# A two-layer graph network on one core: layer 0's sums taken node by node over pairs of tiles, and the first chunk of stage three normalised ahead of the barrier

## The chip, the core and the metric

The kernel runs on one core of a Trainium2 chip. Time is device microseconds (us) of one execution. Of the core's engines TensorE (PE, with its weight loads as PEld) multiplies matrices into PSUM, VectorE (DVE), ScalarE (ACT) and GpSimd (POOL) do the rest, and SyncE (SP) issues most of the DMAs.

## The reference

3125 nodes with 128 features, 103125 edges sorted by destination, everything in float32. Two layers follow each other:

```python
h = relu(layernorm(x))
# layer 0
neighbour = h[dst] @ W_N.T + b_N
agg = segment_sum(neighbour * exp(-edge_weight)[:, None], src)
x = x + relu(h @ W_S.T + b_S + agg)
# layer 1
h = relu(layernorm(x))
q, k, v = h @ Wq + bq, h @ Wk + bk, h @ Wv + bv
logits = sum(q[dst] * k[src], -1) / sqrt(128)
out = elu(softmax per dst (logits) weighted sum of v[src] + h @ Ws + bs)
x = x + out
```

## The kernel before, in words

The nodes are cut into 25 tiles of 128 (NT = 25). Both layers work on dense blocks. For each destination tile the kernel builds two 128 x 3200 tables, one with the number of edges between each pair of nodes and one with the sum of the weights exp(-w) over those edges. The counts serve layer 1 as a mask, the weights serve layer 0 as a matrix.

**Stage one** loads the inputs, normalises x, writes the edges as records and gathers them in windows. It isn't touched, but for the place of one bias.

**Stage two** is the long loop over destination tiles t = 0 to 24. A tile has two halves, called quads (u = 0, 1). For each quad DVE writes one-hot matrices (`quad`, L902 the key, L905 the low part, L908 three products), double-buffered: quad q waits until PE has finished the groups of quad q - 2. PE turns them into counts and weight sums in eight groups a tile (`pe_group`, L1158 and L1160: eight cells of three bfloat16 matmuls each), ACT evacuates each group (`evacuate`, L612 the counts to `gst`, L614 the weights to `wst`), and SP stores the counts to memory. The weights of tile t then go through layer 0 while the groups of later tiles run:

- PE transposes them in seven pieces of four node tiles, the last of one (`pe_turn`, L1121, 25 transposes a tile), ACT copies each piece to `wsb`, which holds two pieces (`act_piece`, L596).
- PE multiplies: `pe_product` (L1131) holds the tile's neighbour features (`hvb`, copied by ACT, L589) as weights, and streams the piece of up to 512 columns. The result is feature by node.
- DVE adds each piece to the running sum `kT` (`dve_piece`, L845), seven adds a tile. The bank is free for the next product but one after that.

The sum starts from h @ W_S.T + b_S, computed up front by `pe_self` (L1108) and moved to `kT` by ACT with the bias (`act_self`, L576). The order is written out by hand. PE does, for each j = 0, 2, 4, 6: two groups, then products of the tile before (`pe_products`), then turns of the tile before (`pe_turns`). DVE's adds for tile t - 2 stand between the one-hot operations of tile t (`dve_tile`). PE, ACT and DVE each run this as a hardware loop of two tiles a pass, with the first and last tiles written out.

At the end `dve_last_tile` adds the last tile's pieces, and once the first two are in, PE transposes the sums of the first five node tiles back to node by feature (`turn_sums`, L1138), and DVE adds them to x and takes the statistics of the next layernorm (`statistics`, L857 to L865). Then all five engines meet (`end_stage`, L180). Each has the slow path (the Else branch, not taken here) between its fast path and this meeting.

**Stage three** handles five chunks of five node tiles: ACT takes the root (`root`, L676), DVE the inverse (`inverse`, L874, L876), POOL scales and shifts into `xn` (L479, L481), PE transposes (L1266), ACT applies relu (L691), and PE projects to keys, values, queries and skip (L1255, L1260). After its transposes of chunk d PE turns the sums of chunk d + 2 (`turn_sums`). Keys and queries go through the same PSUM pair, values and skip through another.

**Stage four** is the attention over all pairs of tiles (L1292 scores, L1303 values), which isn't touched.

## Time and profile before

| | us |
|---|---|
| median of 3 runs | 850.38 (849.42 to 850.85) |
| the profiled execution | 843.88 |
| its span, first to last instruction | 842.10 |
| stage two, main loop (tiles 3 to 24) | about 110 to 450 |
| meeting of the engines, end of stage two | about 470 |
| stage four begins | about 508 |

| engine | busy in the span |
|---|---|
| PE | 759.0 (90%) |
| PEld (weight loads) | 654.6 (78%) |
| DVE | 742.9 (88%) |
| ACT | 494.8 (59%) |
| POOL | 255.0 (30%) |

Durations come from one profiled execution, whose own time stands in the second line. Rows of the timeline and of the chain are merged: "x8" is eight instructions one behind the other. The end of a matmul is modelled and lies some 0.16 us behind the start of the next one in a stream, so that rates are read from start to start.

### The profile page before, as it was taken

The numbers are of one execution on the slowest core, as the hardware profiler recorded it, in microseconds if no ns is written. First come the engines' busy times: TensorE is split into PE (matmuls) and PEld (weight loads), VectorE is DVE, ScalarE is ACT, GpSimd is POOL, SyncE is SP. The second block draws the span as 40 slices with busy tenths as digits, with TensorE's granted clock in tenths as the row PEclk, the third lists the DMA queues.
The fourth block names the chain that finished last, engine by engine and source line by source line (L and its number), as shares of the span: only waits on it lengthen the run. The fifth ranks groups of instructions, "written<-read, shape, count | busy, mean of one in ns | idle before, by whom it ended". The sixth has DMA issues, their size and how long they took to land.

```text
span 842.1 us, 22919 instructions
## 1 busy us (share of the span) xinstructions
PE 759.0 (90%) x8798; PEld 654.6 (78%) x8798; DVE 742.9 (88%) x914; ACT 494.8 (59%) x1013; POOL 255.0 (30%) x206
## 2 busy tenths in 40 slices
PE   0278999999999999999998688899999999999996
PEld 0166777777777777777775467899999999999996
DVE  6785999999999999999994548999999999999971
ACT  4879667677676776776774251535545544545534
POOL 4772000000000000000000320655665765765756
PEclk9999999999999999999999799999999999999999
DMA  9821223123132132131131612223343342342400
GB/s 261 264 78 80 81 92 144 78 107 126 78 126 107 78 138 95 78 156 78 78 156 79 249 66 79 79 81 100 146 162 94 149 162 93 150 162 92 152 7 11
DMA packets 17661, 96.63 MB, mean 115 GB/s; under 512 B 2610, under 2 KB 8860, under 8 KB 11100
## 3 DMA queue, kind: packets, MB, share of 16 engines
q1 hardware_dynamic: 14572, 90.02, 28.1%
q0 software_dynamic: 3056, 6.17, 2.9%
q8 instruction: 21, 0.34, 0.2%
q14 instruction: 12, 0.10, 0.0%
HBM read 51.55 MB, written 44.63 MB: 114 GB/s over the span
## 4 chain that ended last, share of the span: by engine, by line
PE 72%; DVE 12%; issue 10%; ACT 5%; DMA 1%; DVEq 1%; POOL 0%; POOLq 0%; ACTq 0%; PEldq 0%; PEld 0%
PE bank L1303 18%; PE bank L1292 16%; PE bank L1131 14%; PE bank L1121 6%; PE bank L1160 5%; DVE oh_key L908 5%; PE bank L1158 5%; DVE kT L845 3%; PE bank L1289 3%; PE bank L1255 2%; ACT kT L550 1%; PE bank L1260 1%; PE bank L1098 1%; DVE junk L755 1%; ACT qT L539 1%
## 5 line engine op out<-in xcount | busy, mean ns | idle before, releaser
L489 POOL TENSOR_TENSOR sm<-sm,mbc 128x768 f32<-128x768 f32 x100 | 174.3, 1776 | 98.0 <-ACT mbc L710 98.0
L1131 PE MATMUL bank<-wsb,hvb 128*128 128x512 f32 (+1 forms) x350 | 165.2, 577 | 13.7 <-DVE kT L845 12.5
L1158 PE MATMUL bank<-oh_key,oh_lo 128*128 128x100 bf16 x1600 | 170.5, 208 | 1.9 <-ACT wst L614 1.9
L1160 PE MATMUL bank<-oh_key,oh_lo 128*128 128x50 bf16 x3200 | 170.8, 187 | 0.0
L1160 PEld LDWEIGHTS bank<-oh_key,oh_lo 128*128 128x128 bf16 x3200 | 163.8, 97 | 1.1
L1292 PE MATMUL bank<-qT,kT 128*128 (+1 forms) x1250 | 161.4, 278 | 1.2 <-DVEq L180 1.2
L1158 PEld LDWEIGHTS bank<-oh_key,oh_lo 128*128 128x128 bf16 x1600 | 155.8, 97 | 7.7 <-issue 5.5
L1292 PEld LDWEIGHTS bank<-qT,kT 128*128 128x128 f32 x1250 | 157.6, 195 | 3.9 <-DVEq L180 1.3
L1303 PE MATMUL bank<-vals,sm 128*128 128x129 f32 x1250 | 155.0, 281 | 0.0
L1303 PEld LDWEIGHTS bank<-vals,sm 128*128 128x128 f32 x1250 | 151.0, 196 | 0.1
L596 ACT COPY wsb<-bank 128x512 f32<-128x512 f32 (+1 forms) x175 | 88.0, 553 | 106.5 <-PE bank L1121 106.5
L908 DVE TENSOR_TENSOR oh_key<-oh_key,xt 128x1600 bf16<-128x1600 bf16 x150 | 140.8, 994 | 0.0
L714 ACT ACTIVATE sm<-sm 128x768 f32<-128x768 f32 x100 | 89.4, 894 | 85.2 <-POOL sm L489 85.2
L612 ACT ACTIVATE gst<-bank,tiny_col 128x400 f32<-128x400 f32 x200 | 122.9, 614 | 15.4 <-PE bank L1160 12.0
L471 POOL MEMSET vals<- 128x25 f32 x1 | 0.1, 142 | 402.3 <-PEq L180 402.3
L845 DVE TENSOR_TENSOR kT<-kT,bank 128x512 f32<-128x512 f32 (+1 forms) x175 | 105.4, 625 | 13.7 <-PE bank L1131 11.5
L905 DVE TENSOR_TENSOR oh_lo<-xt,lo_tab 128x4096 bf16<-128x4096 bf16 x50 | 115.3, 2306 | 0.0
L991 DVE TENSOR_TENSOR sm<-bank,gl_sb 128x768 f32<-128x768 f32 x100 | 102.0, 1021 | 4.5 <-PE bank L1292 3.3
L1121 PEld LDWEIGHTS bank<-ident,wst 128*128 128x128 f32 x625 | 82.0, 193 | 30.7 <-issue 30.0
L1131 PEld LDWEIGHTS bank<-wsb,hvb 128*128 128x128 f32 x350 | 56.4, 189 | 59.3 <-DVE kT L845 33.1
L614 ACT COPY wst<-bank 128x400 f32<-128x400 f32 x200 | 101.3, 506 | 0.0
L1042 DVE TENSOR_REDUCE mx<-sm 128x128 f32<-128x3328 f32 x25 | 90.5, 3620 | 0.9
(125 smaller groups left out, 740.8 us busy)
## 6 DMA issues: line engine op xcount, KB each, us to landing
gt<-gst SPq DMA_DIRECT2D x25, 1600.0 KB, 5.6
gl_sb<-gt SPq DMA_DIRECT2D x25, 1600.0 KB, 6.7
records<-rec SPq DMA_DIRECT2D x1, 2015.0 KB, 8.2
out<-res SPq DMA_DIRECT2D x24, 64.0 KB, 1.5
src_i<-in_src SPq DMA_DIRECT2D x1, 403.0 KB, 5.8
w_in<-in_edge_weight SPq DMA_DIRECT2D x1, 403.0 KB, 6.3
dst_i<-in_dst SPq DMA_DIRECT2D x1, 403.0 KB, 6.8
dstn_i<-in_dst_next SPq DMA_DIRECT2D x1, 403.0 KB, 7.1
```

The costliest lines, as they stand in the source:

```text
L489: pool.tensor_tensor(part, part, top, ALU.subtract).then_inc(sub_done, 1)
L612: nc.scalar.activation(place, counts, ACT.Ln, bias=tiny_col[:, 0:1], scale=EULER).then_inc(evacs, 1)
L845: V.tensor_tensor(kT[:, cols], kT[:, cols], ps(6 + at)[:, 0:n * P], ALU.add).then_inc(l0_add, 1)
L905: V.tensor_tensor(oh_lo[:, u, :, :, :], along(F_LO, P), table(lo_tab, P), ALU.is_equal).then_inc(onehot, 1)
L908: V.tensor_tensor(block(1 + w), block(0), along(F_W + w, KEYS), ALU.mult).then_inc(onehot, 1)
L991: V.tensor_tensor(twos(v, a, n).rearrange("p k d i -> p k i d"), score_bank(g)[:, 0:n * P].rearrange("p (k i d) -> p k i d", d=P, i=2), gl ...
L1121: ins = T.transpose(ps(4 + at)[:, h * P:(h + 1) * P], tile, ident[:])
L1131: T.matmul(ps(6 + at)[:, 0:n], hvb[:, w, :], wsb[:, at, 0:n], start=True, stop=True).then_inc(l0_mm, 1)
L1158: T.matmul(cells, lo, oh_key[:, u, m, 0:2 * KEYS, i], start=True, stop=False, skip_group_check=True)
L1160: ins = T.matmul(cells[:, KEYS:2 * KEYS], lo, oh_key[:, u, m, (1 + w) * KEYS:(2 + w) * KEYS, i], start=False, stop=w == 2, skip_group_chec ...
L1292: ins = T.matmul(score_bank(g)[:, j * P:(j + 1) * P], kT[:, (a + j) * P:(a + j + 1) * P], qT[:, bass.ds(t * P, P)], start=g < LIFT, stop=T ...
L1303: ins = T.matmul(ps(4 + v % 2)[:, 0:D + 1], weights, vals[:, h, :], start=h == 0, stop=h == NT - 1)
```

## The change

The weights' transposed pieces become the stationary operand, one node tile at a time, and the neighbour features `hv` the moving one, so that the sum comes out node by feature. Two source tiles are accumulated in PSUM, and DVE adds once for both. `wsb` now holds two whole tiles (one lies in `qT`, unused in this stage). The self product is the first matmul of the first pair's accumulation, and its bias a row that DVE adds with it. `hvb`, `act_self`, `act_hv`, `pe_self` and `turn_sums` go. The order of the slots is written in three tables: `TURNS`, `SUMS` and `ADDS`, by parity of the tile. Root, inverse and POOL's normalising of chunk 0, and the statistics of chunk 1, stand ahead of the meeting. The query product gets a PSUM pair of its own.

```diff
+TURNS = (((0, 1), (2, 3), (4, 5), (6,)), ((0, 1), (2, 3), (4, 5), (6,)))
+SUMS = ((None, 0, 1, 2), (3, 4, 5, 6))
+ADDS = (((4, 5), (6, None)), ((0, 1), (2, 3)))
...
-        wsb = sb(s2, "wsb", [P, 2, 4 * P])
-        hvb = sb(s2, "hvb", [P, 2, D])
+        wsb1 = sb(s2, "wsb1", [P, NP])
+        wsb = (qT, wsb1)
...
@@ gpsimd
+            normalise_chunk(0)
+            end_stage(pool, 2)
+            pool.memset(vals[:, :, D:D + 1], 1.0)
+            pool.memset(gl_sb[:, :, NT * P:NTP * P], -FLOOR).then_inc(pad_ready, 1)
+            for d in range(1, NC):
+                normalise_chunk(d)
...
@@ scalar
-            def act_piece(s, w, j):
-                n = PC[j][1] * P
+            def act_piece(s, w, j, q):
+                a, n = PC[j][0], PC[j][1] * P
                 at = (w + j) % 2
                 act.wait_ge(turned, NPC + 1 + NPC * s + j + 1)
-                act.wait_ge(l0_mm, NPC * s + j + 1)
-                nc.scalar.copy(wsb[:, at, 0:n], ps(4 + at)[:, 0:n]).then_inc(l0_ev, 1)
+                act.wait_ge(l0_mm, NPC * (q + 1) + j + 1)
+                nc.scalar.copy(wsb[w][:, a * P:a * P + n], ps(4 + at)[:, 0:n]).then_inc(l0_ev, 1)
...
                         if isinstance(t, int) and t == 0 and j == 7:
-                            act_self(0, 4)
                             take_windows(3, 5)
-                        if isinstance(t, int) and t == 1 and j == 1:
-                            act_self(4, NPC)
-                            act.wait_ge(s_hvb, len(TG))
...
+            root(0)
+            end_stage(act, 2)
...
-                nc.scalar.activation(qT[:, cols], pair(2)[:, 0:CW], ACT.Identity, bias=bcol[:, 3:4],
+                nc.scalar.activation(qT[:, cols], pair(0)[:, 0:CW], ACT.Identity, bias=bcol[:, 2:3],
...
@@ vector
+            def add_sum(q, j, first=False):
+                a, n = PC[j]
+                dve.wait_ge(l0_mm, 2 * NPC + NPC * q + j + 1)
+                part, rows = ps(6 + j % 2)[:, 0:n * P], kt3[:, a:a + n, :]
+                if first:
+                    V.tensor_tensor(rows, part.rearrange("p (t f) -> p t f", f=D),
+                                    brow[:, 3:4, :].to_broadcast([P, n, D]), ALU.add).then_inc(l0_add, 1)
+                else:
+                    dve.wait_ge(l0_add, 3 + NPC * q + j)
+                    flat = kT[:, a * P:(a + n) * P]
+                    V.tensor_tensor(flat, flat, part, ALU.add).then_inc(l0_add, 1)
...
-            def dve_last_tile():
+            def dve_last_tile(q):
                 for j in range(NPC):
-                    dve_piece(NT - 1, 0, j)
-                    if j == 2:
+                    add_sum(q, j)
+                    if j == 3:
+                        dve.wait_ge(l0_add, NPC + 2 + NPC * q + 2)
                         statistics(0)
+                    if j == NPC - 2:
+                        inverse(0)
+                dve.wait_ge(l0_add, NPC + 2 + NPC * q + 3)
+                statistics(1)
...
                     V.tensor_tensor(block(0), along(F_KEY, KEYS), table(key_tab, KEYS), ALU.is_equal).then_inc(onehot, 1)
-                    for j in pieces:
-                        dve_piece(t - 2, v, j)
+                    early, late = ADDS[v][u] if p is not None else (None, None)
+                    if early is not None:
+                        add_sum(p, early, first)
                     V.tensor_tensor(oh_lo[:, u, :, :, :], along(F_LO, P), table(lo_tab, P), ALU.is_equal).then_inc(onehot, 1)
+                    if late is not None:
+                        add_sum(p, late, first)
                     dve.wait_ge(onehot, (t * 2 + u) * HOTS + 1)
                     for w in range(3):
                         V.tensor_tensor(block(1 + w), block(0), along(F_W + w, KEYS), ALU.mult).then_inc(onehot, 1)
-                    for j in later:
-                        dve_piece(t - 2, v, j)
...
+                dve_tile(2, 0, None)
+                dve_tile(3, 1, 0, first=True)
+                dve_tile(4, 0, 0, first=True)
+                dve_tile(5, 1, 1)
+                with dve.Fori(3, NT // 2) as i:
+                    dve_tile(i * 2, 0, i - 2)
+                    dve_tile(i * 2 + 1, 1, i - 1)
+                dve_tile(NT - 1, 0, NT // 2 - 2)
                 for j in range(NPC):
-                    dve_piece(NT - 2, 1, j)
-                dve_last_tile()
+                    add_sum(NT // 2 - 1, j)
+                dve_last_tile(NT // 2)
...
@@ tensor
+            def pe_sum(q, j, parts, first=False):
+                a, k = PC[j]
+                if first and j == 0:
+                    pe.wait_ge(s_hnev, len(TG))
+                    pe.wait_ge(s_hvb, len(TG))
+                pe.wait_ge(l0_add, NPC + 2 + NPC * q + max(j - 1, 0))
+                for s, w in parts:
+                    pe.wait_ge(l0_ev, 2 + NPC * s + j + 1)
+                for h in range(k):
+                    cols = slice((a + h) * P, (a + h + 1) * P)
+                    to = ps(6 + j % 2)[:, h * P:(h + 1) * P]
+                    if first:
+                        T.matmul(to, hT[:, cols], wts[:, WS_, :], start=True, stop=False, skip_group_check=True)
+                    for n, (s, w) in enumerate(parts):
+                        ins = T.matmul(to, wsb[w][:, cols], hv[:, bass.ds(s, 1), :].rearrange("p t f -> p (t f)"),
+                                       start=n == 0 and not first, stop=n == len(parts) - 1, skip_group_check=True)
+                ins.then_inc(l0_mm, 1)
...
+                        if p is not None and SUMS[v][j // 2] is not None:
+                            pe_pair(p, SUMS[v][j // 2], first)
                         if before:
-                            pe_products(t - 1, 1 - v, j)
-                            pe_turns(t - 1, 1 - v, j)
+                            pe_turns(t - 1, 1 - v, TURNS[v][j // 2])
...
+                pe_tile(0, 0, None, before=False)
+                pe_tile(1, 1, None)
+                pe_tile(2, 0, 0, first=True)
+                pe_tile(3, 1, 0, first=True)
+                with pe.Fori(2, NT // 2) as i:
+                    pe_tile(i * 2, 0, i - 1)
+                    pe_tile(i * 2 + 1, 1, i - 1)
+                pe_tile(NT - 1, 0, NT // 2 - 1)
+                for d in range(NG):
+                    pe_pair(NT // 2 - 1, SUMS[1][d])
+                    pe_turns(NT - 1, 0, TURNS[1][d])
+                for j in range(NPC):
+                    pe_sum(NT // 2, j, [(NT - 1, 0)])
...
-                if d + 2 < NC:
-                    turn_sums(d + 2)
...
-                pe.wait_ge(proj_a, d * 2 + 1)
-                across(2, WQ_, q_mm)
+                across(0, WQ_, q_mm)
```

In words: in an even tile PE's four slots sum nothing and then pieces 0, 1, 2 of a pair, in an odd tile pieces 3 to 6. The last tile, 24, has no partner and is summed alone.

## Rows read from the trace of the kernel before

**Rows 1.** The page: busy time of the engines; shares of the last-ending chain.

```profile
PE 759.0 (90%) x8798; PEld 654.6 (78%) x8798; DVE 742.9 (88%) x914; ACT 494.8 (59%) x1013; POOL 255.0 (30%) x206
PE 72%; DVE 12%; issue 10%; ACT 5%; DMA 1%; DVEq 1%; POOL 0%; POOLq 0%; ACTq 0%; PEldq 0%; PEld 0%
```

**Rows 2.** Stretches: us, then busy us and instructions of each engine, clock, DMA.

```profile
187.80:218.95 31.15, 30.27 (x464) 23.74 (x463) 30.97 (x35) 21.83 (x48) 0.00 (x0) 1.00 0.25 105
```

**Rows 3.** Timeline of DVE in the loop: start, us, engine, line, operation, count.

```profile
255.95 0.98 DVE L902 TENSOR_TENSOR oh_key<-xt,key_tab 128x1600 bf16<-128x1600 bf16 x1
256.86 1.28 DVE L845 TENSOR_TENSOR kT<-kT,bank 128x512 f32<-128x512 f32 x2
258.05 2.28 DVE L905 TENSOR_TENSOR oh_lo<-xt,lo_tab 128x4096 bf16<-128x4096 bf16 x1
260.25 2.79 DVE L908 TENSOR_TENSOR oh_key<-oh_key,xt 128x1600 bf16<-128x1600 bf16 x3
```

**Rows 4.** The last-ending chain in the loop: start, us, what.

```profile
259.70 1.80 PE bank L1131 x4
261.50 0.90 PE bank L1121 x8
...
263.99 1.82 PE bank L1131 x4
265.83 0.70 DVE kT L845
```

**Rows 5.** Timeline of PE in stage four.

```profile
604.17 2.84 PE L1292 MATMUL bank<-qT,kT 128*128 x24
606.85 3.23 PE L1303 MATMUL bank<-vals,sm 128*128 128x129 f32 x26
609.91 0.27 PE L1313 MATMUL bank<-ident,mx 128*128 128x128 f32 x1
```

**Rows 6.** Timelines of PE, ACT and DVE in tiles 0 to 2.

```profile
69.79 3.87 PE L1108 MATMUL bank<-hT,wts 128*128 128x512 f32 x8
...
109.78 0.27 PE L1121 MATMUL bank<-ident,wst 128*128 128x128 f32 x1
...
74.28 3.21 ACT L582 COPY xt<-bank 128x640 bf16<-128x640 bf16 x5
...
73.10 2.79 DVE L908 TENSOR_TENSOR oh_key<-oh_key,xt 128x1600 bf16<-128x1600 bf16 x3
84.14 0.99 DVE L902 TENSOR_TENSOR oh_key<-xt,key_tab 128x1600 bf16<-128x1600 bf16 x1 [8.26 <-PE bank L1160]
```

**Rows 7.** Timelines of PE, DVE and POOL at the end of stage two.

```profile
437.20 0.21 PE L1158 MATMUL bank<-oh_key,oh_lo 128*128 128x100 bf16 x1
...
450.94 0.68 PE L1131 MATMUL bank<-wsb,hvb 128*128 128x512 f32 x1
...
461.63 0.82 DVE L857 SCALAR_TENSOR_TENSOR xs<-bank,xs 128x640 f32<-128x640 f32 x1 [1.61 <-PE bank L1138]
...
463.95 1.25 DVE L845 TENSOR_TENSOR kT<-kT,bank 128x512 f32<-128x512 f32 x2
...
466.32 0.30 PEld L1131 LDWEIGHTS bank<-wsb,hvb 128*128 128x128 f32 x2 [0.86 <-ACT wsb L596]
...
470.49 0.87 PE L1138 MATMUL bank<-ident,kT 128*128 128x128 f32 x3 [3.69 <-PEq L180]
...
472.46 1.25 POOL L481 TENSOR_TENSOR xn<-xn,ln_c 128x640 f32<-128x640 f32 x1
...
473.77 1.33 PE L1266 MATMUL bank<-ident,xn 128*128 128x128 f32 x5 [1.98 <-POOL xn L481]
...
475.95 1.89 PE L1255 MATMUL bank<-hc,wts 128*128 128x512 f32 x4
```

**Rows 8.** DMA queues from 150 to 440 us, then from 440 to 480.

```profile
q1 hardware_dynamic: 2676, 30.57, 25.3%
...
q8 instruction: 4, 0.07, 0.8%
```

More of the change, by code:

```diff
@@ L468, in _, with normalise_chunk @@
                 start_slow(pool)
-            end_stage(pool, 2)
-            pool.memset(vals[:, :, D:D + 1], 1.0)
-            pool.memset(gl_sb[:, :, NT * P:NTP * P], -FLOOR).then_inc(pad_ready, 1)
-            for d in range(NC):
+            def normalise_chunk(d):
                 pool.wait_ge(ln_done, d + 1)
@@ L623, in act_tile @@
                         if isinstance(t, int) and t == 0 and j == 7:
-                            act_self(0, 4)
                             take_windows(3, 5)
-                        if isinstance(t, int) and t == 1 and j == 1:
-                            act_self(4, NPC)
-                            act.wait_ge(s_hvb, len(TG))
-                        if before and j == 1:
-                            act_hv(t - 1, 1 - v)
-                        if before and j % 2 == 1:
-                            for piece in range(j - 1, min(j + 1, NPC)):
-                                act_piece(t - 1, 1 - v, piece)
+                        if p is not None and j % 2 == 1:
+                            for piece in TURNS[v][j // 2]:
+                                act_piece(t - 1, 1 - v, piece, p)
                 act_features(0, 3)
@@ L671, in _ @@
                 act_turn(NT - 1, 0)
-            end_stage(act, 2)
             def root(d):
@@ L908, in quad, with dve_tile @@
                         V.tensor_tensor(block(1 + w), block(0), along(F_W + w, KEYS), ALU.mult).then_inc(onehot, 1)
[L909 to L914 removed]
+                def dve_tile(t, v, p, first=False):
+                    quad(t, v, 0, p, first)
+                    quad(t, v, 1, p, first)
                 open_windows(0)
@@ L961, in _ @@
                     next_numbers(f_dnum, FD)
-                with dve.Fori(0, NT // 2) as i:
-                    for w in range(2):
-                        for j in range(NPC):
-                            dve_piece(i * 2 + w, w, j)
-                dve_last_tile()
+                for j in range(NPC):
+                    add_sum(0, j, first=True)
+                with dve.Fori(1, NT - 1) as s:
+                    for j in range(NPC):
+                        add_sum(s, j)
+                dve_last_tile(NT - 1)
             end_stage(dve, 2)
-            V.tensor_scalar(bcol[:, 3:4], bcol[:, 1:2], float(D) ** -0.5, None, ALU.mult).then_inc(s_qb, 1)
-            inverse(0)
-            statistics(1)
+            V.tensor_scalar(bcol[:, 2:3], bcol[:, 0:1], float(D) ** -0.5, None, ALU.mult).then_inc(s_qb, 1)
             for d in range(NC):
@@ L1162, in pe_group, with pe_pair, pe_turns, pe_tile @@
                     ins.then_inc(groups, 1)
-                def pe_products(s, w, j):
-                    for piece in range(max(j - 2, 0), min(j, NPC)):
-                        pe_product(s, w, piece)
-                def pe_turns(s, w, j):
-                    if j == 0:
-                        pe.wait_ge(evacs, 4 + (s + 1) * 2 * SLOTS0)
-                    for piece in range(j, min(j + 2, NPC)):
-                        pe_turn(s, w, piece, True)
-                def pe_tile(t, v, before, two_before):
+                def pe_pair(p, j, first=False):
+                    pe_sum(p, j, [(p * 2, 0), (p * 2 + 1, 1)], first)
+                def pe_turns(s, w, pieces):
+                    for j in pieces:
+                        if j == 0:
+                            pe.wait_ge(evacs, 4 + (s + 1) * 2 * SLOTS0)
+                        pe_turn(s, w, j, True)
+                def pe_tile(t, v, p, before=True, first=False):
                     for j in range(0, SLOTS0, 2):
@@ L1233, in _, with pe_tile_slow @@
                         pe.drain().then_inc(fs_mm, 1)
-                def pe_tile_slow(s, w, uses, last=False):
+                def pe_tile_slow(s, w, uses, first=False):
                     pe.wait_ge(fs_wl[w], uses * 16 + 16)
@@ L1240, in pe_tile_slow @@
                         if j >= 1:
-                            pe_product(s, w, j - 1)
-                        if last:
-                            pe_last(j)
-                with pe.Fori(0, NT // 2) as i:
+                            pe_sum(s, j - 1, [(s, w)], first)
+                pe_tile_slow(0, 0, 0, first=True)
+                pe_tile_slow(1, 1, 0)
+                with pe.Fori(1, NT // 2) as i:
                     pe_tile_slow(i * 2, 0, i)
                     pe_tile_slow(i * 2 + 1, 1, i)
-                pe_tile_slow(NT - 1, 0, NT // 2, last=True)
+                pe_tile_slow(NT - 1, 0, NT // 2)
             end_stage(pe, 2)
-            turn_sums(1)
             def across(i, w, done):
```

120 lines of the change are left out of this document (24 added, 96 removed).

## Prediction

> **What bounds the kernel now.** I read the page first: TensorE (PE) is busy for 90% of the span and holds 72% of the chain that ended last, VectorE (DVE) 12% [rows 1]. The share of 90% hides which engine decides in stage two, so next came the stretch table. Two tiles take 31.15 us, PE is busy for 30.27 and DVE for 30.97 of it [rows 2]: DVE is full, PE has 0.88 us to spare. The timeline of DVE says what fills it, from start to start [rows 3]: in a half tile ("quad") the key one-hot 0.91, the low one-hot 2.20, three products 2.70, together 5.81 us, and 0.60 for each sum of 512 columns (256.86 to 258.05 is two). A tile has two quads (11.62) and seven sums (six of 0.60 and one of 128 columns, about 0.20: 3.8), that is 15.4 of 15.58. The chain gives PE's parts [rows 4]: two products 1.80 (L1131, two instructions a piece, so 0.90 each), eight transposes 0.90, and 16 cells of one-hot matmuls from 262.40 to 263.99, 1.59. A tile of PE work is 4 x 1.59 + 25 transposes (2.81) + six products of 0.90 and one of 0.3 (5.7) = 14.87. The missing 0.71 is PE standing before a product until DVE has freed a bank.
>
> **The change, part by part.**
> *Sums.* Per source tile, seven products of up to 512 columns become 25 of 128, each of two instructions, and their weights (the turned piece) are loaded anew each time. That shape does not stand in L1131; the nearest row is L1292, also float32, 128 columns, weights loaded each time and the moving side at an address from a register: 24 instructions from 604.17 to 606.85, 0.1117 us each. L1303, with 129 columns, accumulating and with strided weights, took 3.06/26 = 0.1177 [rows 5]. A quarter of a 512-column instruction (0.45, rows 4) is 0.1125. So the lower end is 0.1117 and the upper 0.1177; a gain is excluded, since the same columns stream. I take 0.1117: it has the same column count. A pair piece (two tiles, four nodes' tiles) is 16 instructions, S = 1.79; the last piece 0.45. Two tiles cost 50 x 2 x 0.1117 = 11.17 for 11.4 before: for PE the swap is free. The first pair carries the self product too: 24 instructions, 2.68 a piece, last 0.67.
> A rule of the Trainium skill speaks against it: "TensorE: Matmul & The Clock Gate", section Back-to-back issue gap, puts sustained loads and matmuls at about 81 ns for 128 columns and 131 ns for 512. By that four narrow ones cost 2.5 times one wide one, and the sums would rise from 5.7 to some 14 us a tile, 200 us in all; the rows of 0.1117 against 0.45 disagree, and they are this kernel's own type and shape.
> *DVE.* It adds once for two tiles: 11.62 + 1.9 = 13.5 us a tile. It stops being the bound, and PE at (12.72 + 11.17 + 5.62)/2 = 14.76 us becomes it, if nothing stalls. What is late next: the adds stand in DVE's queue ahead of the one-hots that PE needs. Write a pass of the loop in slots of groups G, sum S, turns T. After S1, DVE starts its add 0.20 later, adds 0.60, multiplies 2.70, and with 0.19 to land PE may start the next quad 3.69 us after S1; PE has T 0.90 + G 1.59 + S2 1.79 + 0.11 = 4.39 to do: no stall. After S3: 5.18, no stall. After S5 PE has only 0.90 + 1.59 + 0.45 + 0.11 = 3.05: it stands 0.64 us at the start of each even tile. A pass is 29.51 + 0.64 + 0.04 (hand-overs, eight of 0.005) = 30.19 for 31.16 (two of 15.58): 0.97 gained, ten passes (i = 2 to 11): **9.7 us**. Bounds: no stall at all, 16 us; 0.1177 for each of the 100 instructions takes 0.6 a pass back, which leaves 3.7.
> ACT does the same copies less 0.33 us a tile, at 70% busy; its new wait (a piece of the pair before must be summed) is met a tile ahead. Nothing.
> *Start.* Now tile 0 ends in four self products (69.79, 3.7 us), and ACT's copies of them stand before its window copies (74.28) [rows 6]; tile 1 waits for the other three, and DVE stands 8.26 us until 84.14. New: after 69.8 the window transposes follow ACT's five copies of 0.64 from 70.96, until 73.5. Tile 1 has no sums: 4 G + turns = 9.2, to 82.8. DVE starts quad (2,0) when G of slot 1 ends, 77.9, and is ready at 83.9; PE waits 1.1. Tile 2: 9.2 + 3 x 2.68, to 101.2. Tile 3: 9.2 + 3 x 2.68 + 0.67, to 119.2, and 0.4 of the stall above: tile 4 starts at 119.6. Before: 109.89 (tile 3) + 15.58 = 125.47. **5.9 us**, for the sums of a tile and a half are owed until the end. Bounds 4 and 7.
> *Tile 24.* Before 437.20 to 450.94, 13.74. New 4 x 1.59 + 3 x 0.90 + 2 x 1.79 = 12.64: **1.1**.
> *Tail and barrier.* Before, from 450.94 to the first projection at 475.95: 25.0 [rows 7]. PE's last loads start at 466.32, and its next operation at 470.49: everyone waits 3.7 us for PE, in which instructions are fetched (the queue of rows 8), over the jump past the slow path. Then come root, inverse, two POOL passes (to 473.71), transposes, relu. New, from the last G: four sums of 1.79 or less and 0.11 + 2.81 of turns, 10.5; single sums of 0.90 each: S0 to S5 run to 16.0. DVE adds piece 3 at 15.0, then does the statistics of chunk 0 (461.63 to 463.95, 2.4 us), and only at 18.1 has added piece 4, for which the last sum waits. PE issues it at 18.15 and, with the 3.9 of before from last load to drain, arrives at 22.05. DVE: add 5 18.7, inverse 19.2, add 6 19.5, statistics of chunk 1 to 21.9. POOL: 19.3 + 2.6 = 21.9. All three arrive together at 22.1, 2.8 later than before (19.3), but the chunk is ready: transposes at 22.3, as slow as now (ten, the sums' five among them, take 2.18 from 473.77 to 475.95, so 1.1), relu 0.7, projection at 24.35. **0.65 gained**; the barrier work is moved rather than removed. Bounds: the low clock lasting one product longer costs 1.1; a shorter fetch gains nothing, since DVE and POOL stand at 21.9; so -1 to +1.
> *Rest of stage three.* The sums' transposes (0.55 a chunk) lie beside ACT's relu, which PE waits for afterwards anyway. The query product gets a bank of its own; it hardly waited before, since the key's eviction (about 0.8) lies beside the value products (ten of 0.11). The loads of the counts are issued at the same barrier. Nothing. Stage four is untouched.
>
> **Sum.** 5.9 + 9.7 + 1.1 + 0.65 = 17.35 us off a span of 842.10; the profiled execution took 843.88 (1.8 outside the span), so 826.5. The runs' median, 850.38, lies 6.5 above that execution; the same difference gives **833.0 us**.
>
> **Rivals.**
> (a) *Narrow sums dearer, or the stall larger.* 0.1177 instead of 0.1117 over 1250 + 50 instructions is 7.8 us: 841. For it: L1303 accumulates as these do. Against: it has a column more and strided weights. Chance 0.15.
> (b) *The stall after S5 isn't there*, as DVE runs further ahead or lands sooner: ten passes x 0.64 = 6.4, 826.5. Chance 0.10.
> (c) *Slower: the loop outgrows PE's instruction buffer.* From 150 to 440 us no instruction block is fetched, with some 463 loads and 464 matmuls in the 31 us of a pass [rows 2, 8]; around 440 to 480 four are. The new pass has 534 of each, and no loop of this kernel of that size runs twice. If it doesn't fit, each jump back costs a fetch like the one at the barrier, 3.4 to 3.9 us: ten of them are 37, for 870 us. It decides from a pass costing 1 us more. The Trainium skill, "Runtime: NRT & Kernel Launch", section Instruction fetch mechanics, says that prefetch is sequential and that a taken branch to a page not at hand forces a fetch; by its 128 KiB or 2048 instructions for PE the 1068 of a pass would fit (an estimate). The trace agrees that a jump can stall PE (3.7 us) and that a loop of some 925 doesn't. Chance 0.04.
> (d) *No change*: the sums cost so much more that all is given back. That needs 17.35/1300 = 0.013 us on each instruction, 0.125; no 128-column float32 stream in rows 5 is near it. 0.04, and 0.02 for still slower.
> Forecast 0.65.
>
> **Range and chances.** Own range 829 to 838; with (a) and (b) 826 to 842. A measurement tells 0.2%, 1.7 us, from no change. Faster 0.90, within 0.2% 0.04, slower 0.06.
>
> **What would show it.** Two tiles of the loop in 30.2 us with DVE busy for 27 and PE for 29.6; a gap of PE of some 0.6 us at the start of even tiles only, ended by the one-hot products; L1131's successor at 0.112 us from start to start; tile 4 starting at 119.6, the last groups ending near 434, the first projection near 458.6; a PE gap of about 4 us (not two) before chunk 0's transposes, with POOL's two passes ahead of it. It is wrong if the pass is over 31 us, if PE's gap comes at each quad, or if instruction blocks are fetched within the loop.

## The result, and the profile after

The changed kernel takes 844.26 us (843.27 to 846.04, five runs), the kernel before 850.85 beside it (849.42 to 851.91, five runs): ratio 0.9925, 95% interval 0.9908 to 0.9942. It is faster, by 6.6 us where 17.35 were forecast, and it lies outside the range of 826 to 842.

The page of the changed kernel: busy time, the queue of instruction fetches (packets, MB, share), shares of the last-ending chain.

```profile
PE 755.1 (90%) x9709; PEld 732.8 (87%) x9709; DVE 699.6 (83%) x830; ACT 485.8 (58%) x981; POOL 253.9 (30%) x206
q8 instruction: 27, 0.44, 0.2%
PE 83%; ACT 6%; DVE 5%; issue 2%; another core or an unknown queue 1%; DMA 1%; POOLq 1%; POOL 0%; DVEq 0%; ACTq 0%
```

Against [rows 1], DVE has 43 us less to do and falls from 12% to 5% of the chain, PE rises from 72% to 83%. The bound has moved as forecast; the time has not moved with it. The span is 842.5 us against 842.10, but the first one-hot group starts at 61.78 instead of 55.30. That is not the change: in later profiles the repeated changed kernel starts it at 55.60 and the repeated kernel before at 61.09. Counted from the first group, before takes 786.70 us and after 780.62, 6.08 less, which agrees with the medians. By stages (starts of PE's instructions; tile 24 up to its first sum behind the groups, the tail from there to the first projection):

| stretch | before | after | gained | forecast |
|---|---|---|---|---|
| first group to tile 4 | 70.18 | 64.38 | 5.80 | 5.9 |
| tiles 4 to 23, ten passes | 311.72 | 308.52 | 3.20 | 9.7 |
| tile 24 | 13.74 | 12.89 | 0.85 | 1.1 |
| tail and meeting | 25.01 | 27.18 | -2.17 | 0.65 |
| chunk 0, first projection to query | 2.84 | 4.43 | -1.59 | 0 |
| query of chunk 0 to the end | 363.21 | 363.22 | 0 | 0 |

The first row and the last but one aren't the same in every execution. In the repeated pair (b_again less a_again) 4.1 is gained to tile 4 and nothing is lost in chunk 0's projections, while the loop, tile 24 and the tail come out within 0.1 as here, and the whole gives 6.0.

The loop. One pass in the view by windows (us, then busy us and instructions of PE, PEld, DVE, ACT, POOL, clock, DMA share, GB/s), to be held against [rows 2]:

```profile
280.49:311.36 30.87, 30.34 (x535) 30.07 (x535) 27.48 (x28) 21.51 (x47) 0.00 (x0) 1.00 0.25 106
```

DVE is down to 27.48 of 30.87 (forecast 27), the instructions are the 534 forecast, and PE is busy for 30.34 where 29.6 were forecast. The timeline of PE at the end of an odd tile, and of DVE beside it, tells why (groups left out):

```profile
274.80 0.47 PE L1129 MATMUL bank<-hv,qT 128*128 x2
275.10 0.39 PE L1129 MATMUL bank<-hv,wsb 128*128 x2
275.32 0.39 PE L1129 MATMUL bank<-hv,qT 128*128 x2
...
276.67 1.06 PE L1111 MATMUL bank<-ident,wst 128*128 128x128 f32 x8
277.56 0.21 PE L1144 MATMUL bank<-oh_key,oh_lo 128*128 128x100 bf16 x1
...
279.69 0.27 PE L1111 MATMUL bank<-ident,wst 128*128 128x128 f32 x1
280.49 0.22 PE L1144 MATMUL bank<-oh_key,oh_lo 128*128 128x100 bf16 x1 [0.53 <-ACT wst L611]
```

```profile
276.95 0.69 DVE L837 TENSOR_TENSOR kT<-kT,bank 128x512 f32<-128x512 f32 x1 [1.47 <-PE bank L1129]
277.56 2.79 DVE L907 TENSOR_TENSOR oh_key<-oh_key,xt 128x1600 bf16<-128x1600 bf16 x3
```

The sum piece takes 276.67 - 274.80 = 1.87 for sixteen instructions, not 1.79. The rate is right (275.10 to 275.32 is two at 0.11), but the first two behind the groups take 0.30 instead of 0.22: the stream has a start of 0.08. The transposes behind the sum take 0.89, as before. And PE stands from 279.80 or so to 280.49, once a pass: DVE adds at 276.95, then multiplies until about 280.3. The releaser named is an ACT evacuation that ends 0.07 ahead; that it was DVE, e1_adds shows below.

The end of stage two: timelines of DVE, PE and POOL, to be held against [rows 7].

```profile
463.22 0.82 DVE L848 SCALAR_TENSOR_TENSOR xs<-kT,xs 128x640 f32<-128x640 f32 x1
...
465.54 1.25 DVE L837 TENSOR_TENSOR kT<-kT,bank 128x512 f32<-128x512 f32 x2
466.25 0.49 PE L1129 MATMUL bank<-hv,qT 128*128 128x128 f32 x2 [1.73 <-DVE kT L837]
...
467.17 1.25 POOL L480 TENSOR_TENSOR xn<-xs,ln_c 128x640 f32<-128x640 f32 x1 [392.48 <-DVE ln_c L867]
467.21 1.89 DVE L848 SCALAR_TENSOR_TENSOR xs<-kT,xs 128x640 f32<-128x640 f32 x1
468.50 1.72 POOL L482 TENSOR_TENSOR xn<-xn,ln_c 128x640 f32<-128x640 f32 x1
...
472.57 1.33 PE L1246 MATMUL bank<-ident,xn 128*128 128x128 f32 x5 [5.83 <-POOLq L185]
...
474.75 2.50 PE L1235 MATMUL bank<-hc,wts 128*128 128x512 f32 x4 [0.85 <-ACT hc L679]
```

POOL's drains (two meetings each; ns least, median, most; first and last start) in the kernel before and in the changed one, then PE's clock behind the meeting by windows:

```profile
L180 POOLq DRAIN  x2: 1363/4002/6641, 63.7 to 496.6; - x2
L185 POOLq DRAIN  x2: 1363/2706/4049, 468.5 to 497.2; - x2
```

```profile
469.50:479.70 10.20, 6.28 (x20) 4.66 (x21) 4.18 (x24) 1.80 (x3) 4.31 (x5) 0.50 0.60 226
```

PE issues its last sum 18.68 after the start of the tail (forecast 18.15) and would arrive near 22.6. DVE's first step of the statistics takes 1.89 beside POOL where the same step for chunk 0 takes 0.82 alone (463.22), POOL's second pass 1.72 instead of 1.25, and POOL's drain, begun with that pass at 468.5, lasts 4.05: it ends 2.3 us after the pass, and everybody goes on at 472.54. Those 2.3 us belong to this drain and not to the passes ahead of it. The first drain that a kernel gives POOL ends 2.30 us after POOL's last instruction in all thirteen profiles; in the kernel before it runs from 63.7 to 70.4, behind an instruction that ends at 68.06, when nobody waits for POOL. The second one, behind two passes of the same shape (the 1363 ns), ends 0.07 after them. The change has moved the late drain from a place where it cost nothing to the meeting. The meeting is over at +24.97 instead of +22.1. From there to the projection it is 2.2, as forecast. Then the low clock (0.50, the 1.2 GHz level, 10.2 us long as before) covers all the projections of chunk 0 instead of the last transposes and the first 1.1 us of the projections.

### The profile page after: what moved, and what is told of

It reads as the page before. It is cut to its first block, busy times and chain, and to the rows that moved or that the text cites. A ratio compares the mean times of both kernels' runs of the same rounds, so it can differ in the third digit from the quotient of the medians.

```text
span 842.5 us, 24371 instructions
## 1 busy us (share of the span) xinstructions
PE 755.1 (90%) x9709; PEld 732.8 (87%) x9709; DVE 699.6 (83%) x830; ACT 485.8 (58%) x981; POOL 253.9 (30%) x206
## 4 chain that ended last, share of the span: by engine, by line
PE 83%; ACT 6%; DVE 5%; issue 2%; another core or an unknown queue 1%; DMA 1%; POOLq 1%; POOL 0%; DVEq 0%; ACTq 0%
PE bank L1280 18%; PE bank L1129 16%; PE bank L1269 16%; PE bank L1146 9%; PE bank L1144 8%; PE bank L1111 8%; PE bank L1266 3%; PE bank L1235 2%; PE bank L1240 1%; ACT kT L558 1%; ACT wst L611 1%; ACT gst L609 1%; DVE junk L743 1%; PE bank L1097 1%
## 5 line engine op out<-in xcount | busy, mean ns | idle before, releaser
L480 POOL TENSOR_TENSOR xn<-xs,ln_c 128x640 f32<-128x640 f32 x5 | 7.8, 1563 | 405.9 <-DVE ln_c L867 405.9
L1129 PE MATMUL bank<-hv,qT 128*128 (+1 forms) x650 | 128.3, 285 | 2.0 <-DVE kT L837 2.0
L1129 PE MATMUL bank<-hv,wsb 128*128 (+1 forms) x600 | 116.0, 275 | 0.0
L1129 PEld LDWEIGHTS bank<-hv,qT 128*128 128x128 f32 x650 | 96.7, 191 | 2.5 <-DVE kT L837 2.3
L837 DVE TENSOR_TENSOR kT<-kT,bank 128x512 f32<-128x512 f32 (+1 forms) x84 | 52.7, 629 | 49.4 <-PE bank L1129 48.3
L1129 PEld LDWEIGHTS bank<-hv,wsb 128*128 128x128 f32 x600 | 91.1, 192 | 0.0
```

The lines of the kernel that those rows point to most:

```text
L1129: ins = T.matmul(to, wsb[w][:, cols], hv[:, bass.ds(s, 1), :].rearrange("p t f -> p (t f)"), start=n == 0 and not first, stop=n == len(par ...
```

## Experiments

The ratios are against the kernel before, run beside each (its medians were 844.75, 845.24 and 850.59 in the three sets). "First group to the end" is from the profile: 786.70 before, 780.62 after.

**a_again** is the changed kernel unaltered, with the first set.

> The changed kernel again, unaltered, as the yardstick on this chip. Its profile also tells whether the 6.5 us by which the first group of tile 0 came later than in the profile of the kernel before (61.78 against 55.30, ACT's first window copy 6.5 us late) belong to the change or vary from execution to execution. If they vary: 0.992 to 0.993 of the kernel before, and a first group at either about 55.8 or 61.8. If they belong to the change: 61.8 every time, and never in a profile of the kernel before. Loop pass 30.87 us, projection of chunk 0 at the low clock.

838.05 us, ratio 0.9917 (0.9903 to 0.9931); first group to the end 780.53, ten passes 308.50. In the two profiles of the changed kernel the loop and the tail (27.18) agree, and their medians differ by 6.2, the place of the first group. Other stretches differ and make up for one another: here the granted clock is 0.50 for 3.4 us in tile 0, which lasts 19.50 instead of 17.85 (so too in four of the nine variants below), chunk 0's projections take 3.85 instead of 4.43, and a stretch of low clock in stage four is missing.

**e1_adds**: the even tile's add of piece 5 moved to the second quad.

```diff
-ADDS = (((4, 5), (6, None)), ((0, 1), (2, 3)))
+ADDS = (((4, None), (5, 6)), ((0, 1), (2, 3)))
```

> The changed kernel with DVE's add of piece 5 moved one quad later, next to that of piece 6 (ADDS for even tiles ((4, None), (5, 6))). My theory: the 0.70 us for which PE stands once a pass comes from this add, for which the one-hot products of quad (even, 0) wait in DVE's queue. Then the pass falls from 30.87 to 30.17 and the time by 7 us, to 0.984 or 0.985 of the kernel before. Rival one: PE stands for DVE's own length (the one-hots take what they take), then the gap only moves to the next quad and the time stays at 0.9925. Rival two: the gap is PE's loop and register work at the start of a pass; then nothing moves either.

830.77 us, ratio 0.9828 (0.9811 to 0.9844). One pass by windows:

```profile
300.00:330.16 30.16, 30.16 (x536) 30.07 (x535) 27.48 (x27) 21.51 (x48) 0.00 (x0) 1.00 0.26 109
```

Ten passes take 301.61: 0.69 a pass less, with PE busy all the way. Only DVE's order was changed, so PE had waited for DVE's products, queued behind an add whose sum comes late. The stall was what the forecast made it (0.70 for 0.64). What remains between 30.16 and the forecast's stall-free 29.55 is 0.61 a pass, about eight starts of 0.08.

**e5_turns_first** swaps sums and transposes within each slot.

```diff
-                        if p is not None and SUMS[v][j // 2] is not None:
-                            pe_pair(p, SUMS[v][j // 2], first)
                         if before:
                             pe_turns(t - 1, 1 - v, TURNS[v][j // 2])
+                        if p is not None and SUMS[v][j // 2] is not None:
+                            pe_pair(p, SUMS[v][j // 2], first)
```

> The changed kernel with the transposes ahead of the sums in each slot of PE, else the same. Theory (a start cost of the float32 128-column stream after the bfloat16 groups, 0.08 us once a slot): the first transposes after a group take 0.98 for eight, the sums behind them 1.79 for sixteen, so a slot with both costs as much as before; the slot's sum ends 0.98 later, by which the one-hot products that stand behind DVE's add come later too, so the stall at the even tile grows from 0.70 to about 1.6, and perhaps new ones of up to 0.3 after S1 or S3; a pass 31.8 instead of 30.87, all in all 9 to 12 us over the changed kernel, ratio to before 1.003 (1.000 to 1.008). Rival (the 0.08 belongs to the sums: loads of turned weights or the moving side at a register's address): the sums take 1.87 in this order too and the transposes 0.90, the slot again as long. Only the durations tell the two apart, not the total.

850.19 us, ratio 1.0064 (1.0042 to 1.0086). Timeline of PE, one slot:

```profile
304.01 1.15 PE L1111 MATMUL bank<-ident,wst 128*128 128x128 f32 x8
305.00 0.39 PE L1129 MATMUL bank<-hv,qT 128*128 x2
305.22 0.39 PE L1129 MATMUL bank<-hv,wsb 128*128 x2
...
306.79 0.21 PE L1144 MATMUL bank<-oh_key,oh_lo 128*128 128x100 bf16 x1
```

Now the transposes take 0.99 for eight and the sum 1.79: the 0.08 goes to whichever stream follows the groups, and the rival falls. A pass takes 32.04, as the sum that DVE waits for ends later (forecast 31.8). The order of a slot alone is worth 1.4%.

**e9_split** is e1_adds with the sum between the two groups of a slot, so that PE goes from groups to a 128-column stream 15 times a pass, not 8.

```diff
                         pe_group(t, j)
+                        if p is not None and SUMS[v][j // 2] is not None:
+                            pe_pair(p, SUMS[v][j // 2], first)
                         pe_group(t, j + 1)
-                        if p is not None and SUMS[v][j // 2] is not None:
-                            pe_pair(p, SUMS[v][j // 2], first)
```

> e1_adds with each sum moved from behind the two groups of its slot to between them (group, sum, group, transposes). The work of every engine is the same; what changes is how often TensorE goes from the bfloat16 groups to a float32 stream of 128 columns: 15 times a pass of two tiles instead of 8 (seven slots of eight have a sum). Theory (each such change costs 0.08 us at its first instructions): the sum takes 1.87 and the eight transposes behind the second group 0.98 instead of 0.90, so a pass takes 30.16 + 7 x 0.08 = 30.7, over the loop, tiles 2 and 3 and tile 24 some 6 us more than e1_adds; ratio to before 0.990 (0.988 to 0.992). Rival (the 0.08 is paid once a slot whatever its order, for the waits or the addresses from a register at its sum): the pass stays at 30.16 and the ratio at 0.983.

855.47 us, ratio 1.0054 (1.0038 to 1.0070). Timeline of PE (groups left out), then of DVE at the start of a quad:

```profile
303.30 0.47 PE L1129 MATMUL bank<-hv,qT 128*128 x2
303.61 0.39 PE L1129 MATMUL bank<-hv,wsb 128*128 x2
...
305.97 1.15 PE L1111 MATMUL bank<-ident,wst 128*128 128x128 f32 x8
```

```profile
302.62 0.99 DVE L898 TENSOR_TENSOR oh_key<-xt,key_tab 128x1600 bf16<-128x1600 bf16 x1 [1.78 <-PE bank L1146]
```

The durations came out as expected: 1.87 for the sum (next group at 305.17) and 0.98 for the transposes behind the second group, both in one slot. The total did not: a pass takes 31.82, 1.66 over e1_adds, of which 7 x 0.08 = 0.56 are starts. The rest is two new waits of PE: 0.8 before a sum, until DVE has added, and 0.2 before a group. The slot's last group ends a sum later, and DVE may write the next quad's key one-hot only then (it stands 1.78 at 302.62), so its adds slip too. My 0.990, missed by 1.5%, had counted no such wait.

**b_again** is the kernel before once more.

> The kernel before once more, to see where its first one-hot group of PE starts and how long the rest takes: 55.3 in its profile and 61.8 in that of the changed kernel. If the place varies from execution to execution and belongs to neither kernel (theory), this one may start at 55 or at 61 with the same way of 786.8 from there to the end; if the change had moved it (rival), it starts at 55 in every run of the kernel before and at 61 in every run of the changed one, which the repeated changed kernel (55.6) has already put in doubt.

849.47 us; first group at 61.09 and 786.5 from there to the end, ten passes 311.70. So the place of the first group belongs to neither kernel. It also shows how the old loop stood to these starts (timeline of PE, groups left out; the four instructions of the wide stream, 312.08 to 313.46, each in a window of its own):

```profile
304.29 0.47 PE L1131 MATMUL bank<-wsb,hvb 128*128 128x128 f32 x2
304.59 1.06 PE L1121 MATMUL bank<-ident,wst 128*128 128x128 f32 x8
...
312.08 0.68 PE L1131 MATMUL bank<-wsb,hvb 128*128 128x512 f32 x1
312.60 0.59 PE L1131 MATMUL bank<-wsb,hvb 128*128 128x512 f32 x1
313.03 0.59 PE L1131 MATMUL bank<-wsb,hvb 128*128 128x512 f32 x1
313.46 0.59 PE L1131 MATMUL bank<-wsb,hvb 128*128 128x512 f32 x1
313.88 1.06 PE L1121 MATMUL bank<-ident,wst 128*128 128x128 f32 x8
```

Behind groups, two products of 128 columns take 0.30 instead of 0.22. Four of 512 take 1.80, and that has the same start in it: from start to start they take 0.51, 0.43, 0.43 and 0.43. The first instruction takes 0.51 in all 57 wide streams behind groups between 130 and 430 us, in the first profile of this kernel as in this one. Both loops therefore pay eight starts of 0.08 a pass. What differs is the rate: a wide instruction is 0.429, or 0.107 for 128 columns, against the narrow one's 0.112.

**e8_extra**: e1_adds with two more adds of 512 columns on DVE in each quad, into a buffer that nothing reads.

```diff
+                    if p is not None and not first:
+                        for k in range(2):
+                            dve.wait_ge(extra, (t * 2 + u - 10) * 2 + k + 1)
+                            V.tensor_tensor(hc[:, 0:4 * P], hT[:, 0:4 * P], hT[:, 0:4 * P], ALU.add).then_inc(extra, 1)
...
```

> e1_adds (changed kernel without the even tile's stall) with two more adds of 512 columns on DVE in each quad from tile 5 on, into a buffer that nothing needs: 8 a pass, 0.6 us each, 4.8 us of DVE work, which makes 27.5 + 4.8 = 32.3 a pass, more than PE's 30.2. Theory (DVE was the bound of the loop before and PE is now, with 2.7 us of DVE to spare a pass): the pass becomes 32.3 to 32.5, DVE the bound again, 2.2 a pass over ten passes, about 22 us more than e1_adds, ratio to before near 1.009 (1.004 to 1.014). Rival (DVE never bound the loop, PE and the order of its waits did, and the gain of the change came from elsewhere): the extra work is hidden and the ratio stays at 0.983 to 0.987.

858.32 us, ratio 1.0155 (1.0134 to 1.0177), more than expected, as each add took 0.66, not 0.60. One pass by windows:

```profile
300.00:332.78 32.78, 30.57 (x537) 29.95 (x533) 32.23 (x36) 21.38 (x47) 0.00 (x0) 1.00 0.24 100
```

With 8 x 0.66 = 5.3 us more to do, DVE is full again (32.23 of 32.78) and PE waits. DVE's work does set the loop once it passes PE's 30.2, and only the 2.7 us of its slack were free: a pass grows by 2.6.

**e2_behind** undoes the second part of the change: root, inverse, normalising of chunk 0 and statistics of chunk 1 stand behind the meeting.

```diff
@@ gpsimd, behind the meeting
-            for d in range(1, NC):
+            for d in range(NC):
@@ vector, behind the meeting
+            inverse(0)
+            statistics(1)
...
```

> The changed kernel with the second part of the change undone: root, inverse and POOL's normalising of chunk 0 and the statistics of chunk 1 stand behind the meeting again, the sums stay as changed. I sized this part at -1 to +1 us. My theory after the traces: ahead of the meeting it makes DVE and POOL the last to arrive (POOL's drain ends 2.3 us after its last pass) where PE arrived last before, so that it is worth 1 us at most: meeting over at about 470.2 instead of 472.5 (with a first group at 61.8), POOL's passes then 2.7 more, first transposes at 473.7, and 0.993 to 0.994 of the kernel before. Rival: normalising ahead hides the 3.5 us of root, inverse and passes in full, and without it the time is 3 to 4 us longer, 0.9965.

839.87 us, ratio 0.9941 (0.9927 to 0.9956). Timeline of PE:

```profile
459.17 0.49 PE L1126 MATMUL bank<-hv,qT 128*128 128x128 f32 x2 [1.73 <-DVE kT L836]
466.69 1.30 PE L1243 MATMUL bank<-ident,xn 128*128 128x128 f32 x5 [7.04 <-POOL xn L482]
```

The meeting is over at 462.65, when PE's sequencer is there, 2.8 earlier in the tail than in the changed kernel, but the tail as a whole takes 28.36 instead of 27.18. So the second part gains 1.2 us of tail (the medians lie 1.8 us apart the same way, with intervals that just overlap), and the first part loses 3.35 there against [rows 7]'s 25.01: the tile and a half of sums, owed since the start, stands there, and PE's last sum is issued at +18.7 where it was +15.4.

**e3_pool_first** lets POOL signal its arrival ahead of chunk 0.

```diff
+            pool.drain().then_inc(stage_end, 1)
             normalise_chunk(0)
-            end_stage(pool, 2)
+            pool.wait_ge(stage_end, 5)
```

> The changed kernel, only that POOL drains and signals its arrival before it normalises chunk 0 (its first chunk), and then waits for the other engines; all else as in the changed kernel. Theory (POOL's drain behind two busy passes, 2.3 us past their end, is what the other engines wait for): the meeting is over when PE arrives, at 25.3 - 1.0 = 24.0 to 24.4 us after the last group instead of 25.1, released by PE's sequencer, and the transposes of chunk 0 follow at once, since POOL's passes are done by then: 0.7 to 1.1 us gained, ratio 0.9905 against 0.9917 for the changed kernel, within the intervals. Rival (DVE's statistics of chunk 1, stretched beside POOL, are as late): the transposes come at 25.0 as before.

842.35 us, ratio 0.9898 (0.9882 to 0.9915). Timelines of DVE and PE:

```profile
468.91 1.90 DVE L849 SCALAR_TENSOR_TENSOR xs<-kT,xs 128x640 f32<-128x640 f32 x1
...
472.50 0.93 PEld L1247 LDWEIGHTS bank<-ident,xn 128*128 128x128 f32 x5 [4.25 <-DVEq L185]
```

The tail takes 25.40, 1.78 less, more than the 0.7 to 1.1 expected. The late drain was the price; now DVE ends last, still stretched to 1.90. The medians can't tell this run from the changed kernel (0.9898 and 0.9917, with overlapping intervals); the tail of the profile can.

**e4_both**: e3_pool_first, and DVE's statistics of chunk 1 behind the meeting.

```diff
@@ vector, dve_last_tile
-                dve.wait_ge(l0_add, NPC + 2 + NPC * q + 3)
-                statistics(1)
@@ vector, behind the meeting
+            statistics(1)
```

> The changed kernel with two edits at the end of stage two: POOL signals its arrival at the meeting before it normalises chunk 0, and the statistics of chunk 1 are behind the meeting. My theory: PE's arrival (last sum issued at 466.25, drain at 470.1) is then the last, the meeting ends at about 470.3 instead of 472.5, chunk 0 is ready at 470 as nothing shares DVE's and POOL's time any more, and the transposes start 2.2 us sooner: 0.990. Rival one: the arrival of DVE or ACT holds it at 471.5, 1 us gained, 0.9915. Rival two: the 2.3 us come back since chunk 1's statistics are now late and the clock stays low for as long after; 0.9925.

837.10 us, ratio 0.9896 (0.9878 to 0.9913). Timelines of POOL, ACT and PE:

```profile
463.59 1.25 POOL L482 TENSOR_TENSOR xn<-xn,ln_c 128x640 f32<-128x640 f32 x1
464.99 1.30 PE L1246 MATMUL bank<-ident,xn 128*128 128x128 f32 x5 [3.17 <-POOL xn L482]
467.38 0.30 ACT L663 ACTIVATE ln_c<-mv,eps_col 128x5 f32<-128x5 f32 x1 [6.33 <-SPq L185]
467.58 0.69 ACT L680 ACTIVATE hc<-bank 128x640 f32<-128x640 f32 x1
468.32 2.08 PE L1235 MATMUL bank<-hc,wts 128*128 128x512 f32 x2 [2.02 <-ACT hc L680]
```

Without DVE's statistics beside it POOL's second pass takes 1.25 again, and the transposes start 2.7 earlier in the tail than in the changed kernel. But the root of chunk 1 now waits for those statistics, and chunk 0's relu stands behind it in ACT's queue: 1.2 us are lost again.

**e6_best** joins e1_adds and e4_both, and puts that root behind the relu.

```diff
...
-            root(1)
...
                 nc.scalar.activation(hc[:], pair(1)[:, 0:CW], ACT.Relu).then_inc(hc_ready, 1)
+                if d == 0:
+                    root(1)
```

> The changed kernel with the stall of the even tiles taken away (in the even tile DVE adds piece 4 in the first quad and pieces 5 and 6 in the second, which took 7.0 us off the loop in e1_adds), and with the three edits of the meeting together: POOL signals its arrival before it normalises chunk 0, the statistics of chunk 1 stand behind the meeting, and ACT takes the root of chunk 1 after its first relu instead of before. Theory: the last group to the first projection takes 27.3 us in the changed kernel, of which some 2.3 are POOL's drain and the rest the sharing between DVE and POOL; in e4_both the meeting was over 6.1 us earlier against the last sum and the transposes of chunk 0 2.7 earlier, but ACT's root held the relu back for about 1.2. With all edits the first projection comes 2.5 to 3.5 us earlier after the last group than in e1_adds (27.3), near 24.3, so the ratio to the kernel before is that of e1_adds (0.9828) less 0.3 to 0.4 per cent: 0.979 (0.977 to 0.981). Rival: what is gained ahead of the meeting is given back by the low clock, which then lies in the projections in any case; then 0.982 as e1_adds.

828.13 us, ratio 0.9796 (0.9778 to 0.9814): faster than both kernels, as expected. The tail is 24.62. Timeline of PE:

```profile
452.94 0.49 PE L1130 MATMUL bank<-hv,qT 128*128 128x128 f32 x2 [1.73 <-DVE kT L839]
456.75 1.26 PE L1247 MATMUL bank<-ident,xn 128*128 128x128 f32 x5 [3.32 <-PEq L185]
458.88 2.50 PE L1236 MATMUL bank<-hc,wts 128*128 128x512 f32 x4 [0.88 <-ACT hc L679]
```

The meeting now waits for PE alone, 3.8 us after its last sum.

**e7_warm**: the changed kernel with 14 transposes, read by nobody, ahead of the last sum.

```diff
                 for j in range(NPC):
+                    if j == NPC - 1:
+                        for k in range(14):
+                            T.transpose(pair(1)[:, k % 8 * P:(k % 8 + 1) * P], ident[:], ident[:])
```

> The changed kernel with 14 transposes that nobody reads placed ahead of PE's last sum, in the time in which PE waits there for DVE (1.7 us idle in the changed kernel). In the changed kernel the granted clock falls at 469.5 for 10.2 us and chunk 0's projections run at the low level: 4.43 us from the first key projection to the query projection, 2.84 before. Theory A (the fall follows PE's standing still between the last sum's piece and the meeting, and the short stop before the last sum counts): the fall comes later or not at all ahead of the projections; they take 2.8 and the time falls by 0.2 per cent, 0.990. Theory B (the stop at the meeting, 3.9 us and more, is what matters): the clock falls at the same place, within 1 us, for 10.2 us, and the time stays, or grows by up to 0.5 us where the extra transposes hold the last sum back; ratio 0.992 to 0.993.

837.68 us, ratio 0.9912 (0.9890 to 0.9933), as the changed kernel. PE, then the clock behind the meeting by windows:

```profile
457.78 1.69 PE L1195 MATMUL bank<-ident 128*128 128x128 f32 x14
459.68 0.49 PE L1129 MATMUL bank<-hv,qT 128*128 128x128 f32 x2 [0.20 <-DVE kT L837]
466.00 1.33 PE L1249 MATMUL bank<-ident,xn 128*128 128x128 f32 x5 [5.83 <-POOLq L185]
```

```profile
462.60:472.80 10.20, 5.95 (x20) 4.52 (x21) 4.23 (x24) 1.79 (x3) 4.64 (x5) 0.50 0.59 220
```

With PE idle for only 0.20 ahead of its last sum the clock still falls some 3 us behind that sum, as in the changed kernel: the short stop ahead of the last sum isn't needed for it to fall. That it is the stop at the meeting isn't shown either: in b_again the clock is down from 471.3, 1.1 us before PE's last product, and in e1_adds from about 453, half a microsecond behind the start of the last sum. Clock by windows and PE's last product in b_again:

```profile
471.30:485.00 13.70, 8.39 (x29) 5.80 (x28) 6.51 (x29) 3.64 (x6) 5.59 (x6) 0.50 0.60 230
```

```profile
472.36 0.79 PE L1131 MATMUL bank<-wsb,hvb 128*128 128x128 f32 x2 [0.35 <-ACT wsb L596]
```

Every one of the thirteen profiles has a low stretch of 6.8 to 13.7 us around the meeting (0.50), and its place moves against the work from one execution to another.

## Why the prediction was wrong

*What bounds the kernel.* Right: DVE was full and gave the bound to PE (e8_extra, e1_adds).

*Sums.* This is the step that failed: "Two tiles cost 50 x 2 x 0.1117 = 11.17 for 11.4 before: for PE the swap is free". The two prices were not read alike. Every float32 stream behind bfloat16 groups starts 0.08 late, wide or narrow, and both loops have eight such streams a pass. The old 0.90 a product is an average over a stream of four with its start in it; the new 0.1117 was read in stage four, within a long stream, where no start can show. With the starts on both sides the sums' part of a pass goes from 11.4 to 11.8: the swap costs PE 0.4 a pass (100 x 0.1117 against 24 x 0.429 and 4 x 0.11), where the forecast had it gain 0.2. That is 0.64 a pass, 6.4 us of the 6.5 missing in the loop; the stall's 0.06 more is balanced by hand-overs ("eight of 0.005") that cost nothing. With 0.66 for its starts the forecast's 29.51 is 30.17, and e1_adds, where PE doesn't stand, measures 30.16. The forecast even had the number in hand: "one of 0.3" for the old loop's 128-column product is 0.08 above two of 0.1117, and I didn't ask why.

The rule that spoke against the change (the Trainium skill, "TensorE: Matmul & The Clock Gate", Back-to-back issue gap: 81 ns for 128 columns, 131 for 512) does not explain it. By it the sums would have cost some 200 us more; here the narrow instruction takes 0.112 and the wide one 0.429, and the measurement decides.

*DVE and the stall.* Right in place, cause and nearly in size: 0.70 for 0.64, 6.9 us by e1_adds.

*Start.* Right in mechanism, with some luck in the number: 5.80 for 5.9. Tile 3, for one, took 0.2 more than forecast, for its starts, but tile 1 had begun 0.35 earlier than forecast; and in a_again, with its stretch of low clock in tile 0, the gain is 4.1. *Tile 24:* 0.85 for 1.1, three starts of 0.08 short.

*Tail and barrier.* Wrong in sign: -2.17 for +0.65. That the barrier's wait for PE was "moved rather than removed" was right, and so was PE's part (+22.6 for +22.05). Two terms were missing. POOL's first drain, which now stands here, ends 2.3 us after its pass, where I let POOL arrive with the pass: 1.8 us, by e3_pool_first. And the statistics and POOL's passes, which I had ending together, hold each other up: 1.07 us on DVE's first step, 0.47 on POOL's second pass, both gone ahead of the meeting in e4_both (POOL's pass 1.25) and e6_best. The Trainium skill, "SBUF — State Buffer", SBUF: two separate sides, says that a DVE instruction with two SBUF inputs and a GpSimd one that reads SBUF hold a shared port pair exclusively, whichever starts first. The trace agrees: DVE's step has two such inputs, starts 0.04 behind POOL's pass and takes 1.07 more, about that pass's remainder (1.21); POOL's next pass then takes 0.47 more. Behind the meeting, where DVE's step comes first (473.18), DVE takes 0.82 and it is POOL's pass that takes 1.77. The forecast let the two run beside each other freely.

*Low clock.* I had bounded it at one product, 1.1; it cost 1.59 in this pair of profiles. But the same projections took 3.90 in b_again and 3.85 in a_again, a pair in which it cost nothing. How much of the 1.59 is the change's isn't shown.

*Rest of stage three.* Right: nothing.

*Rivals.* (a) came nearest in time, 841, by a price that is about right for a wrong reason: the rate of 0.1117 held, and with the seven starts that stand at its sums a pass pays 0.1174 an instruction, close to (a)'s 0.1177. (b) is false as it stands, and e1_adds shows what it would have given. (c) is false: between 150 and 440 us there are two instruction blocks, not ten passes' worth. (d) is false as well: 0.1174 is far from its 0.125.

Open is why a float32 stream begins late behind the groups, why POOL's first drain ends late and its others don't, and whether fewer, longer streams a pass would win starts back; neither loop was tried so.

## What to carry to other kernels

Before one price is set against another, see that both were read alike. The average over a short stream has its start in it, and the spacing in the middle of a long stream doesn't; here that difference was larger than the one between the instructions. Read a new instruction's price where it will stand, behind what will precede it. When an engine's work is moved ahead of a meeting of all engines, count its drain and what it shares with whoever works beside it; an engine whose moved work nobody needs before the meeting is over can signal first (e3_pool_first). When the bound moves to another engine, look at once for the one wait that its order leaves, since here a two-number edit was worth as much as the whole change.

## What the hardware showed that I had not expected

- A float32 stream behind bfloat16 groups starts 0.08 us late, whatever its width: the first of 128 columns takes 0.19 instead of 0.11, sums and transposes alike, the first of 512 takes 0.51 instead of 0.43.
- Without that start, 512 float32 columns in one instruction take 0.429 us and four instructions of 128, each with its weights loaded, 0.447: the narrow form costs 4% more.
- The first drain that a kernel gives POOL ends 2.30 us after its last instruction in all thirteen profiles, whatever stands ahead of it, and its later ones 0.07 after.
- DVE's 0.82 becomes 1.89 and POOL's 1.25 becomes 1.72 when both work from SBUF at once.
- In each kernel the first group starts at 55 or at 61 us from one set of runs to another, which moves the median by 6 us: as much as the change.
